# A layer of attention and FFN: the normalized input and output transposed by DMA as 16-bit halves, in place of TensorE

## What is computed

```python
def attention(x, ...):                    # x is the normalized input
    xx = shift_by_one_token(x) - x
    xk, xv, xr, xg = (x + xx * time_maa_m for m in "kvrg")
    r, k, v = xr @ Wr.T, xk @ Wk.T, xv @ Wv.T      # by head
    g = silu(xg @ Wg.T)
    for chunk of 64 tokens:
        att = (rc @ kc) * w_mat
        yc = att @ vc + rc @ state * wb
        state = ws * state + (kc * wk) @ vc
    yn = (y - mean(y)) / sqrt(var(y) + EPS) * gamma + beta    # by head
    return (yn * g) @ Wo.T
x = x + attention(layernorm(x), ...)
x = x + (gelu(half(layernorm(x)) @ W0.T + bias0) @ W1.T + bias1)
```

## Time and profile before

| | |
|---|---|
| median of 3 runs | 2241.5 us (2240.76 to 2241.71) |
| profiled execution | 2242.77 us, span 2240.5 us |
| mean granted TensorE clock | 0.977 of full |
| chain that ended last | PE 90%, DVE 4%, issue 1% |
| HBM | 316 MB read, 25 MB written |
| DMA queue of SP | 433.62 MB, 61.7% of 16 engines' span |

### The profile page before, as it was taken

One profiled execution on the slowest core, in us unless ns is written; L12 is line 12 of the kernel. 1 busy time (PEld: TensorE's weight loads), 2 busy tenths in 40 slices (PEclk: granted clock), 3 DMA queues, 4 the chain that ended last, 5 costly groups with the idle time before them and its releaser, 6 DMA issues.

```text
span 2240.5 us, 63092 instructions
## 1 busy us (share of the span) xinstructions
PE 2133.4 (95%) x26336; PEld 1543.8 (69%) x26336; DVE 1859.6 (83%) x4293; ACT 1077.6 (48%) x1882; POOL 414.0 (18%) x339
## 2 busy tenths in 40 slices
PE   3667999999999999999999999999999999999998
PEld 3455777776777776677777667777776677777664
DVE  4689888889888888898888889888888988888851
ACT  5454455444455544445454544445544445554441
POOL 1211122112122111212211211122121212221120
PEclk7778999999999999999999999999999999999999
DMA  6444576666566666555666756567665656666666
GB/s 198 127 128 166 171 212 204 212 191 183 189 199 213 204 218 201 178 185 197 211 209 212 211 179 184 193 208 212 213 212 180 190 187 205 210 206 203 194 210 213
DMA packets 282666, 437.78 MB, mean 195 GB/s; under 512 B 123536, under 2 KB 160912, under 8 KB 282384
## 3 DMA queue, kind: packets, MB, share of 16 engines
q1 hardware_dynamic: 281952, 433.62, 61.7%
q10 hardware_dynamic: 432, 0.14, 0.0%
HBM read 316.24 MB, written 25.17 MB: 152 GB/s over the span
## 4 chain that ended last, share of the span: by engine, by line
PE 90%; DVE 4%; issue 1%; DMA 0%; ACT 0%; POOL 0%; POOLq 0%; SPq 0%; ACTq 0%; DVEq 0%
PE F L818 20%; PE F L832 20%; PE B L656 11%; PE Y L684 7%; PE B L798 7%; PE sc L656 7%; PE Y L730 4%; PE sc L714 3%; PE T L656 3%; PE T L771 2%; PE Y L747 2%; PE sc L697 1%; DVE mixf L217 1%; PE T L256 1%; PE B L256 1%
## 5 line engine op out<-in xcount | busy, mean ns | idle before, releaser
L818 PE MATMUL F<-xT,ring 128*128 128x256 f16 x4096 | 489.3, 273 | 5.5 <-DMA xT<-xh 5.3
L832 PE MATMUL F<-ring,hT 128*128 128x512 f16 x2048 | 481.9, 379 | 1.2 <-ACT hT L1258 1.2
L818 PEld LDWEIGHTS F<-xT,ring 128*128 128x128 f16 x4096 | 396.5, 98 | 67.5 <-issue 7.2
L832 PEld LDWEIGHTS F<-ring,hT 128*128 128x128 f16 x2048 | 192.9, 98 | 204.0 <-issue 1.5
L1373 POOL TENSOR_TENSOR Shl<-S,Shl 128x512 f16<-128x512 f32 x128 | 180.4, 1410 | 661.0 <-ACT Shl L1226 661.0
L245 ACT ACTIVATE mix<-mixf 128x1024 f16<-128x1024 f32 x128 | 135.3, 1057 | 340.9 <-DVE mixf L217 223.4
L1258 ACT ACTIVATE hT<-F,b,f_rho 128x256 f16<-128x256 f32 x512 | 260.7, 563 | 43.1 <-PE F L818 43.1
L217 DVE SCALAR_TENSOR_TENSOR mixf<-dx,maa,xnT 128x256 f32<-128x256 f32 x512 | 271.6, 555 | 0.0
L656 PE MATMUL B<-mix,WT 128*128 128x256 f16 x2304 | 270.1, 274 | 0.0
L656 PEld LDWEIGHTS B<-mix,WT 128*128 128x128 f16 x2304 | 224.3, 98 | 36.2 <-issue 0.2
L1005 DVE TENSOR_TENSOR att<-att 128x512 f16<-128x512 f32 x256 | 193.9, 796 | 17.9 <-ACT att L1220 17.9
(11 more groups left out here) (163 smaller groups left out, 2964.2 us busy)
## 6 DMA issues: line engine op xcount, KB each, us to landing
ring<-w_dram SPq DMA_DIRECT2D x512, 512.0 KB, 4.1
kx<-kT SPq DMA_DIRECT2D x96, 256.0 KB, 2.7
rx<-rT SPq DMA_DIRECT2D x96, 256.0 KB, 4.2
xa<-in_L_attn_x SPq DMA_DIRECT2D x32, 512.0 KB, 7.5
vbd<-vN SPq DMA_DIRECT2D x256, 64.0 KB, 3.1
x<-in_L_attn_x SPq DMA_DIRECT2D x32, 512.0 KB, 5.2
out<-x SPq DMA_DIRECT2D x32, 512.0 KB, 3.9
ring<-in_L_ffn_W SPq DMA_DIRECT2D x10, 512.0 KB, 6.8
```

Source lines behind the costliest of these rows:

```text
L818: mm = eng.matmul(F[:, j % 2, i * BT:(i + 1) * BT], ring[:, use % RING, i, a * C + kk * P:a * C + (kk + 1) * P], xT[:, :, kk, :], start=(k ...
L832: mm = eng.matmul(F[:, t, :], hT[:, k, rows(t)], ring[:, use % RING, i, a * C:(a + 1) * C], start=(k == 0 and a == 0), stop=(k == NH - 1 a ...
```

## The change

Both transposes leave TensorE. For each, ScalarE splits the 32-bit words into two planes of 16-bit halves (two copies of 128x1024 words of type uint16), SP transposes both planes in one DMA of 128x2048 words, and ScalarE joins them by two copies that write every second 16-bit word. No further memory is taken: the planes of xa lie in dx and, transposed, in mixf; those of y lie in ygT and, transposed, in yg. Values up to 65535 pass through ScalarE's copy unchanged.

The first block's transpose, in the preparation, stays on TensorE. Affine gamma and beta are now applied from ygT to ygT, in SBUF, no longer from PSUM. The order on the engines changes with it:

- ScalarE: the split of y (`act_y_words`) stands ahead of the high half of rT from B. Normalization (`act_norm`) and split of xa (`act_x_words`) come right after that, ahead of `act_mix_hi(n, 3)` and the high half of rT from T. The join of y is in `act_gated`. The join of xa (`act_x_join`) stands behind the first gate, and `act_gated_hi` and the gelu behind it come after the second `act_weights_hi`.
- VectorE: `dve_dx` moves behind the second weighing (`dve_weigh(n, 1)`).
- SP: the transpose of y's words stands behind the one of kN, the transpose of xa's words behind the DMAs of rx.
- Waits: y may be overwritten once it is split, `pe_scores` no longer waits for the affine instructions, `pe_kv` and `pe_G` no longer for the evictions of xnT; the load of the next x waits for the split of xa.

```diff
+    def act_x_words(eng, n):
+        eng.wait_ge(s_xn, NT * (n + 1))
+        eng.wait_ge(s_mix, 4 * n)
+        for h in range(2):
+            eng.activation(x_words[:, h * NT * C:(h + 1) * NT * C].rearrange("p (t c) -> p t c", t=NT),
+                           halves(xa[:, :, :])[:, :, :, h], ACT.Copy).then_inc(s_xw, 1)
+
+    def sp_x_words(eng, n):
+        eng.wait_ge(s_xw, 2 * n)
+        eng.wait_ge(s_ml, 4 * n - 1)
+        eng.dma_start_transpose(x_wordsT.rearrange("p (k t) -> p k t", t=P), x_words).then_inc(s_xwT, 16)
+
+    def act_x_join(eng, n):
+        eng.wait_ge(s_dx, n)
+        eng.wait_ge(s_mix, 4 * n)
+        eng.wait_ge(s_carry, n + 1)
+        eng.wait_ge(s_xwT, 16 * n)
+        src = x_wordsT.rearrange("p (h t g k) -> p h g t k", h=2, t=NT, g=G)
+        dst = halves(xnT[:, :, 1:BT + 1]).rearrange("p g (t k) h -> p h g t k", t=NT)
+        for h in range(2):
+            eng.activation(dst[:, h], src[:, h], ACT.Copy).then_inc(s_xT, 1)
...
-    def pe_yT(eng, n):
...
-            if due(n):
-                eng.wait_ge(s_af, G * n)
...
+    def act_y_words(eng, n):
+        eng.wait_ge(s_yn, NT * (n + 1))
+        if due(NT * n):
+            eng.wait_ge(s_ygl, NT * n)
+        for h in range(2):
+            eng.activation(y_words[:, h * NT * C:(h + 1) * NT * C].rearrange("p (t c) -> p t c", t=NT),
+                           halves(y[:, :, :])[:, :, :, h], ACT.Copy).then_inc(s_yw, 1)
+
     def act_gated(eng, n):
-        eng.wait_ge(s_yT, NT * (n + 1))
-        if due(NT * n):
-            eng.wait_ge(s_ygl, NT * n)
+        eng.wait_ge(s_ywT, 16 * (n + 1))
+        src = y_wordsT.rearrange("p (h t g k) -> p h g t k", h=2, t=NT, g=G)
+        dst = halves(ygT[:, :, :]).rearrange("p g (t k) h -> p h g t k", t=NT)
+        for h in range(2):
+            eng.activation(dst[:, h], src[:, h], ACT.Copy).then_inc(s_yT, 1)
+        eng.wait_ge(s_yT, 2 * (n + 1))
...
+    def sp_y_words(eng, n):
+        eng.wait_ge(s_yw, 2 * (n + 1))
+        if due(NT * n):
+            eng.wait_ge(s_Wo, NT * n)
+        eng.dma_start_transpose(y_wordsT.rearrange("p (k t) -> p k t", t=P), y_words).then_inc(s_ywT, 16)
```

More of the change, by code:

```diff
@@ L145, in program @@
     T32 = T16[:, :].bitcast(F32)
+    x_words = dx[:, :, :].rearrange("p g t -> p (g t)").bitcast(U16)
+    x_wordsT = mixf[:, 0, :, :].rearrange("p g t -> p (g t)").bitcast(U16)
     s_ident, s_const, s_maa, s_tin = (sem(f"s_{v}") for v in ("ident", "const", "maa", "tin"))
@@ L237, in act_xT, with halves @@
                            ACT.Copy).then_inc(s_xT, 1)
+    def halves(fp32):
+        return fp32.bitcast(U16).rearrange("p a (b h) -> p a b h", h=2)
+    def act_x_words(eng, n):
[17 more added lines that the diff above has]
+            eng.activation(dst[:, h], src[:, h], ACT.Copy).then_inc(s_xT, 1)
     def act_mix_hi(eng, n, m):
@@ L686, in pe_V @@
         mm.then_inc(s_pV, 1)
-    def pe_yT(eng, n):
-        p = n - 1
-        if n < nb:
-            eng.wait_ge(s_kl, 2 * n + 2)
-        else:
-            eng.wait_ge(s_am, 8 * nb)
-        for t in range(NT):
-            eng.wait_ge(s_yn, NT * p + t + 1)
-            for g in range(G):
-                tr = eng.transpose(sc[:, t, rows(g)], y[:, t, rows(g)], ident[:, :])
-            tr.then_inc(s_yT, 1)
     def pe_scores(eng, n, c):
@@ L750, in pe_from_state, with pe_kv @@
                         mm.then_inc(s_in, 1)
-    def pe_kv(eng, n, t, ahead):
+    def pe_kv(eng, n, t):
         if t == 0:
-            if ahead:
-                eng.wait_ge(s_xT, NT * (n + 2))
-            else:
-                eng.wait_ge(s_rl, 2 * n + 2)
+            eng.wait_ge(s_rl, 2 * n + 2)
             eng.wait_ge(s_vl, NT * n + 2)
@@ L774, in pe_kv, with pe_G @@
                         mm.then_inc(s_kv, 1)
-    def pe_G(eng, n, half, ahead):
+    def pe_G(eng, n, half):
         if half == 0:
@@ L779, in pe_G @@
             eng.wait_ge(s_rl, 2 * n + 1)
-            if ahead:
-                eng.wait_ge(s_xT, NT * (n + 1) + 1)
         else:
@@ L867, in pe_step @@
             pe_up(eng, n, 1)
[L868 to L869 removed]
         if ff:
             pe_up(eng, n, 2)
[L872 to L876 removed]
+        if att_n:
             pe_prepare(eng, n, "X1")
@@ L881, in pe_step @@
             pe_scores(eng, n, 0)
-            pe_kv(eng, n, 0, ahead)
-            pe_G(eng, n, 0, ahead)
+            pe_kv(eng, n, 0)
+            pe_G(eng, n, 0)
             pe_prepare(eng, n, "G0")
@@ L892, in pe_step @@
         if att_n:
-            pe_G(eng, n, 1, ahead)
+            pe_G(eng, n, 1)
             pe_prepare(eng, n, "G1")
@@ L906, in pe_step @@
         if att_n:
-            pe_kv(eng, n, 1, ahead)
+            pe_kv(eng, n, 1)
         if ff:
@@ L1119, in dve_step @@
             dve_gated(eng, n - 1)
-        if ahead:
-            dve_dx(eng, n + 1)
         if att_n:
@@ L1280, in act_step @@
                 act_piece_square(eng, 1, 6)
+        if tail:
+            act_y_words(eng, n - 1)
+        if att_n:
             act_R_hi(eng, n, 0)
+        if ahead:
+            act_norm(eng, n + 1)
+            act_x_words(eng, n + 1)
+        if att_n:
             act_mix_hi(eng, n, 3)
@@ L1286, in act_step @@
             act_prepare(eng, n, "R1")
-        if ahead:
-            act_norm(eng, n + 1)
         if n == 0:
@@ L1310, in act_step @@
             act_gelu(eng, n, 2)
-        if ahead:
-            act_xT(eng, n + 1)
         if ff:
@@ L1319, in act_step @@
             act_prepare(eng, n, "G0")
+        if ahead:
+            act_x_join(eng, n + 1)
+        if att_n:
             act_state_hi(eng, n, 0)
+            act_weights_hi(eng, n, 1)
+            act_prepare(eng, n, "sc1")
         if tail:
@@ L1470, in sp_step @@
             sp_rx(eng, n)
+        if ahead:
+            sp_x_words(eng, n + 1)
         if n == 0:
```

45 lines of the change are left out of this document (19 added, 26 removed).

## The result

| | before | changed |
|---|---|---|
| median | 2241.1 us (2240.29 to 2241.71, 4 runs) | 2457.1 us (2452.68 to 2457.94, 4 runs) |
| profiled execution | 2242.77 us | 2457.94 us |
| span, mean granted clock | 2240.5 us, 0.977 | 2455.9 us, 0.954 |
| first step's start to the last's, 31 step distances | 2031.3 us | 2236.2 us |

The ratio is 1.0944, 95% interval [1.0931, 1.0957]. The forecast was 2420 us, 37 us less, within a range of 2275 to 2530.

A forecast was written before the change was run, and what follows sets the result against it. TensorE was taken to set the pace. From 2242.8 us, 149 us of longer steps (the 55 saved included) and 28 us of clock loss, less 1.3, gave 2418.5, stated as 2420 us, with a whole range of 2275 to 2530.

The forecast's parts named there:

- What bounds the kernel: TensorE, busy for 95% of the span, sets the pace; VectorE, at 83%, is the one to watch.
- what leaves TensorE: Eight fp32 transposes take 0.88 us; 63 groups make 55 us, or 1.76 us a step.
- Place A: Before the first FFN matmuls: rT of T comes late on ScalarE, VectorE 4.09 us later, TensorE waits 2.96 us.
- Place B: Gated output and moved dx: three GpSimd instructions of about 1.0 us hold VectorE; att x v starts 3.5 us late.
- Places B and C: C is the first down group, waiting for the last gelu, 4.8 us later; B and C together wait 3.6 us.
- The step without clock loss: Each step 4.8 us longer than 64.92 us; over 31 steps 149 us.
- Clock: Idling before the first FFN group brings half-speed stretches: 0.9 us a step, 28 us in all, between 0 and 51.
- What ScalarE gets: Eight copies of 128x1024 16-bit words a step, 0.97 us each, at least 0.47, at most twice the mix row.
- the rival of slow words: A ScalarE copy takes twice the mix row, 5.8 us a step more: 2600 us; chance 8%.
- DMA: SP's two more transposes a step, and the FFN weights issued behind them, cost nothing.
- The condition I named: SP's added transposes cost nothing unless one takes over 8 us.

The follow-up runs named there:

- xbg: Against the kernel before: only xa goes by DMA, y stays on TensorE, and ScalarE's copies leave the chains TensorE waits for; 2227.1 us, ratio 0.9925.
- c_copies: The kernel before plus four ScalarE copies of 128x1024 16-bit words a step, before the first FFN matmuls, no DMA transpose or join; 2345.5 us, ratio 1.0444.
- b_gated: The changed kernel with the gated high half and fifth gelu back ahead of the second high half of the weights on ScalarE; 2460.0 us, ratio 1.0953.
- c_fill: The changed kernel plus 24 useless TensorE matmuls a step, filling the wait before the first FFN group; 2433.8 us, ratio 1.0840.
- c_join: The changed kernel with the two copies joining xa cut to one of 128 tokens' columns each; 2459.4 us, ratio 1.0958.
- c_dma: The kernel before plus two DMA transposes of 512 KB a step on SP that nobody reads; 2265.2 us, ratio 1.0086.
- a_order: The changed kernel, ScalarE reordered before the first FFN group: rT of B, split y, mix, rT of T, normalization, split xa; 2360.5 us, ratio 1.0525.
- c_both: The changed kernel with the order of a_order and GpSimd's two low-half instructions for the gated output cut to one element per partition; 2314.8 us, ratio 1.0309.
- both_new_order: The whole change, all eight copies kept, with ScalarE and VectorE reordered around the first FFN group and the gated output; 2319.7 us, ratio 1.0327.

## Why the prediction was right, point by point

The mechanism was right at all three places. The 37 us that are missing are no single error: several terms were a little too small, and they did not cancel.

- **What bounds the kernel** and **what leaves TensorE**: right. xbg gives 0.87 us a step for one of two sets, where 0.88 was put down.
- **Place A**: right. 2.96 us were forecast, 2.86 measured, by the chain as written: from the end of the normalized y to the end of rT from T, 7.47 us were put down and 7.39 measured. c_copies makes the same gap with four copies and ScalarE's order alone. VectorE waited 4.18 us for rT of T, "about 4" in the prediction.
- **Place B**: right in cause, wrong in one link. GpSimd's three instructions cost VectorE 2.8 us (4.82 - 2.0; 3.0 put down), and cutting two of them gives 71 us. But the move of the gated high half does not bring them there: b_gated has the old order, and VectorE still needs 4.64 us. That the lateness of the whole chain brings them there is what is left, and no run tests it; nor does a run show what the moved dx costs by itself. The rule of the Trainium skill (SBUF — State Buffer, "SBUF: two separate sides"), an exclusive port lock between the two engines, agrees with all three traces: 4.82 us with three GpSimd instructions, 4.64 with the same three in another place, 2.97 with one of full size.
- **Places B and C**: 3.6 us of waits were put down. The step shown has 1.10 + 1.55 at B, and C's wait of 1.09 us comes in part of the steps (15 of them, 14.5 us in all). The sum is nearly right (3.74 us), the division is not: I had not seen that the middle FFN group waits for the gelu of the one two groups earlier.
- **The step without clock loss** was forecast at 64.92 + 4.8 = 69.7 us, and the step from 1433.8, which has every wait and no half clock, takes 70.34. The 0.6 us more are there at place B already. The join of y starts as forecast (30.27 us into the step for 30.16, with the step of the rows starting at 988.4), but VectorE's multiplication by the gate starts 34.95 us into it, where 34.2 were put down. Over 25 steps this is some 15 us.
- **Clock**: mis-sized, but less than it seems. I took 0.9 us a step. A low stretch begins at place A in 18 of 25 steps. The two steps of 72.01 and 70.34 us, with the same four waits, show its price: 1.67 us. That is the 1.65 which the prediction had as the most, so all of it reached place B and none disappeared in the waits. 18 x 1.67 / 25 = 1.20 us a step for the 0.9, 8 us over the 25 steps. (The 18 steps take 72.5 us in the mean and the other seven 70.1, 2.4 less. That is not the clock alone: in five of the seven the gap at A is shorter, 1.76 to 2.65 us.) c_fill shows that the gap brings the low stretch, since no stretch begins there once the gap is filled, and the kernel is faster. The rule of the Trainium skill (TensorE: Matmul & The Clock Gate, "Why this matters for your kernels"), that idle gaps bring the half clock back, agrees with a gap of 2.86 us and then 0.50; the step from 1433.8 has the same gap and stays at 1.00.
- **What the sum left out**: the 25 steps are 29 us above the forecast, and beside the 15 and the 8 some 6 us remain, which go with low stretches behind place B and with the "issue" gaps. The gaps are 16.3 us of idling, but a step that has one often has no wait at C, and the next a shorter one at A, so most of it is made up. The end of the run, behind the last start, takes 10.7 us more than before, which I had not costed: it is 156 to 160 us in every kernel whose y goes by DMA, and 147 to 149 in every other.
- **The first six steps** agree by luck: 33.5 us against 6 x 5.7 = 34. The first two do not have all parts, and the six differ from those of the kernel before by 2.4 to 10.4 us each.
- **What ScalarE gets**: 0.97 for a split was close (2.00 for two). A join is 1.35, far below twice the mix row, so the rival of slow words is out. For xa this costs nothing (c_join). For y the join stands in the chain to B: two copies and the last one's end were put down at 2.04 us and take 2.57 from start to the next start. That agrees with the 0.6 us a step above, but no run tests it.
- **DMA**: costed at nothing, and c_dma shows 20 us in the kernel before, mostly as "issue" gaps. The changed kernel has 16.3 us of them in 25 steps and one wait of 2.6 us for the ring; in a_order, c_both and both_new_order, with shorter steps, waits for the ring come in too. The condition I named (a transpose over 8 us) was the wrong one: they land after 4.3 and 5.6 us. What comes late is the weights behind them, in the faster kernels, and by my reading TensorE's instructions.

The rows of SP's two transposes in the changed kernel, y and xa (ns min/median/max), and their landing:

```profile
L1477 SPq DMA_TRANSPOSE yg<-ygT x32: 1464/1919/2891, 155.7 to 2378.3; - x32
...
DMA to landing us min/median/max: 4.3/4.3/4.6
```

```profile
L258 SPq DMA_TRANSPOSE mixf<-dx x31: 2423/3747/4522, 80.0 to 2245.7; - x31
...
DMA to landing us min/median/max: 4.6/5.6/7.3
```
